# Second attention of a two-layer kernel: the incoming rows are added by GpSimd, not by TensorE

## The chip, the cores and the metric

One core of one Trainium2 chip runs the whole program. The metric is the device time of one execution in microseconds (us), lower is better.

## What is computed

Two layers over 8 x 512 tokens of width 256. Each is an attention and a feed-forward part, both read the same normalised rows, and both are added to the incoming rows. The second layer's attention is a gated linear recurrence over time, run over 4 batches of 1,024 tokens, 8 heads of 32:

```
xn = _layernorm(x, axis=-1)
x = x + _L1_attn_ref(xn, ...) + _L1_ffn_ref(xn, ...)

# in _L1_attn_ref
h = x * rsqrt(mean(x * x) + 1e-06) * norm_w
q, k, v = (heads(Wq), heads(Wk), heads(Wv))        # rope on q and k
beta, ig, og = sigmoid gates per token and head
def step(M, inp):
    M = M * f_t + g_t * scale * (k_t outer v_t)
    y_t = (q_t @ M) * o_t
return einsum('bld,ed->ble', y, Wout) + bout
```

The feed-forward part of the second layer is a mixture of 8 experts of width 1,024 with the two best chosen for each token.

## The kernel before, in words

The engines' queues are written out by hand. A list of steps (`plan2`, built by `shared_order` and `second_order`) is walked by each engine, which takes the steps that are its own. Order between engines is by semaphores, each counted up by its producer.

The second attention runs in chunks of 128 tokens, 32 of them, in the order `ORDER1`: the first chunk of each batch of 512, then the second of each, and so on. One pass over the tuple `TURN` is one turn, and the number behind a kind says which chunk it treats relative to the turn's own. In a turn, TensorE makes the value product (`project_val`, L1823, bank 3), the q/k product of the next chunk (`project_qk`, L1811), turns q and k (`turn`, L1839, and L1847 for the second gated q), makes the state products of the chunk before (`keys`, L1881 and L1887), its causal part (`update`, L1897), the scores (`affinity`, L1865, banks 2 to 5), and last the output projection of the chunk before (`project_out`, L1906 to L1910, bank 1). VectorE makes the rope (L2406, L2417, L2418), scans the decays of a chunk (`decay`, L2426, both inputs in SBUF), weighs the scores with them (`weigh`, L2433, PSUM and one SBUF input) and renews the state (L2445, 16 chunks). ScalarE copies and scales: values (L1369), turned q and k (L1376, L1381), the update's sum (L1387), keys (L1405), and the output sums (`out_copy`, L1410).

The rows `ACC` hold the sums of the first layer, 256 values a token. `project_out` starts its bank with the product identity x `ACC` row (L1906), adds the products with `WOUT` (L1909, after the semaphore `yt_put`, which ScalarE's L1387 gives) and the bias (L1910); ScalarE then writes the bank back into `ACC` and gives `oe_put`. The sync engine stores finished quarters of `ACC` (`store_sums`, L859). After the loop, TensorE's experts wait for all `oe_put`.

GpSimd multiplies the rotated q by the gates (`open`, L1082, and from the ninth chunk on L1088). From the routing on it also scatters the routing table of the experts into DRAM, 64 indirect DMAs (`scatter`, L978), three in a turn from the ninth turn on, put into the step `route`, ahead of `open` in the turn. After the last turn it gathers rows for the experts (`first_rows`, L1005), where `rows` stands in the list ahead of the last `out_copy`. TensorE turns the gathered rows (L1685).

Of the kernel before, what the change touches and what calls it, by code (L numbers as in the profile page):

```python
# [309 lines left out]
def build(nc, t, out):  # L310
    ctx = ExitStack()
    with ctx:
# [144 lines left out]
        WT = view(carve(1024), 1024).rearrange("p (g n) -> p g n", g=2)  # L457
        YT = view(carve(256), 256)
        top[0] = max(top[0], hs_at + 2048)
        FV = view(carve(256), 256)  # L460
# [133 lines left out]
        zero0, zero1 = sem("zero_xs0"), sem("zero_rest")  # L594
        b_in, b_cut, b_rows = sem("b_in"), sem("b_cut"), sem("b_rows")
        b1_turned, b1_put = sem("b1_turned"), sem("b1_put")
# [38 lines left out]
        kd_put, y_made, yt_put, dm_made, m_put = (sem(n) for n in ("kd_put", "y_made", "yt_put", "dm_made", "m_put"))  # L635
        out_made, oe_put, sums_out = (sem(n) for n in ("out_made", "oe_put", "sums_out"))

        xt_ready = {b: [(banks0[f"xt{c}", b][0], banks0[f"xt{c}", b][1] + 1) for c in range(2)] for b in range(NB)}
# [41 lines left out]
        def sync(sp):  # L680
# [113 lines left out]
            for k in range(3):  # L794
                sp.dma_start(B2S[8 * k:8 * k + 8, :], b3[0:8, k, :]).then_inc(b_rows, 16)
            attention_over(sp)
            sp.wait_ge(b_rows, 48)
            sp.wait_ge(b1_turned, 1)
# [58 lines left out]
            def store_sums(c):  # L857
                sp.wait_ge(oe_put, 8 * c + 8)
                sp.dma_start(ov[c], ACC.rearrange("p (b i) d -> p i b d", b=NB)[:, c]).then_inc(sums_out, 16)  # L859
# [55 lines left out]
        def second_over(eng):  # L915
            eng.wait_ge(out_made, NT)
            eng.wait_ge(oe_put, NT)
            eng.wait_ge(m_put, NST)
            eng.wait_ge(w_put, NT)
            eng.wait_ge(slot_turned, 2)  # L920


        def gpsimd(pool):
# [151 lines left out]
            def open_gates(n):  # L1075
# [9 lines left out]
                if n >= NB:  # L1085
                    if n >= NB + 2:
                        pool.wait_ge(e_turned, n - NB - 1)
                    pool.tensor_tensor(h8(QE2[par]), QK2[par][:, 0:8, :], hb(EF[:, i, :]), ALU.mult).then_inc(qe_put)  # L1088

            def bias_split():  # L1090

# [18 lines left out]
            for kind, *a in plan2:  # L1110
                if kind == "sums":
                    sums(*a)
                elif kind == "weights":
                    weights()
                elif kind == "combine" and on_pool(a[0]):
                    combine(*a)
                elif kind == "const1":
                    const1()
                    bias_split()
                elif kind == "gates" and a[1] == 4:  # L1120
                    gates(a[0])
                elif kind == "open":
                    open_gates(*a)
                elif kind == "scatter":
                    scatter(1, *a)
                elif kind == "rows":
                    first_rows(1)
# [6 lines left out]
        def scalar(act):  # L1134
# [273 lines left out]
            def project_out(n):  # L1408
                act.wait_ge(out_made, n + 1)
                act.activation(ACC[:, ORDER1[n], :], ps(1, 256, 512), ACT.Copy).then_inc(oe_put)  # L1410

# [40 lines left out]
        def tensor(pe):  # L1452
# [251 lines left out]
            def expert_down(layer, i):  # L1704
# [5 lines left out]
                if i == 0:  # L1710
                    pe.wait_ge(b_rows, 48)
                    pe.wait_ge(wd_in, 64 + 128 * layer)
# [187 lines left out]
            def project_out(n):  # L1900
# [3 lines left out]
                else:  # L1904
                    pe.wait_ge(const1_set, 12)
                pe.matmul(ps(1, 256, 512), ident, ACC[:, ORDER1[n], :], start=True, stop=False)  # L1906
                pe.wait_ge(yt_put, n + 1)
                for g in range(2):
                    pe.matmul(ps(1, 256, 512), YT[:, 128 * g:128 * g + 128], WOUT[:, g, :], start=False, stop=False)  # L1909
                pe.matmul(ps(1, 256, 512), ones3[0:96, :], BO3[0:96, :], start=False, stop=True).then_inc(out_made)  # L1910
# [653 lines left out]
```

## Time and profile before

| | |
|---|---|
| time, median of 3 runs | 1592.35 us (1588.64 to 1593.25) |
| profiled execution | 1598.56 us |
| span of its trace | 1596.8 us |
| TensorE busy | 1514.8 us (95%) |
| VectorE busy | 847.8 us (53%) |
| ScalarE busy | 746.2 us (47%) |
| GpSimd busy | 706.3 us (44%) |

The span is that of the trace; the profiled execution's own time lies a little above it. In the profile PE is TensorE's matmul, PEld its weight load, DVE VectorE, ACT ScalarE, POOL GpSimd and SPq the queue of the sync engine. L12 is line 12 of the kernel. A matmul in f32 shows as two records, one for each pass. Busy shares are means over stages with different limits, so that a wait is read in its stage. The second attention's turns run from about 860 to 1074 us of the span.

### The profile page before, as it was taken

Reading aid. Unit: us, or ns where it says so; the run is one execution under the profiler, and the core shown is the slowest. Engines: PE = TensorE matmul, PEld = TensorE weight load, DVE = VectorE, ACT = ScalarE, POOL = GpSimd, SP = SyncE. Lnnn points to the kernel's source line nnn. Section 1 sums busy time; section 2 is a strip of 40 time slices with the busy share of each in tenths; the row PEclk is TensorE's granted clock in tenths of the full one; section 3 lists DMA queues with packets and bytes.
Section 4 is the critical chain, followed back from the end, with each engine's and each line's share of the span. In section 5 each row is a group of like instructions: output and inputs, shape, how many; then the busy total and the mean of one; then the engine's idle time right before and its main releaser. Section 6 shows DMA issues by size and latency. Waiting matters only on the chain.

```text
span 1596.8 us, 32512 instructions
## 1 busy us (share of the span) xinstructions
PE 1514.8 (95%) x10874; PEld 1168.8 (73%) x10874; DVE 847.8 (53%) x2400; ACT 746.2 (47%) x1953; POOL 706.3 (44%) x815
## 2 busy tenths in 40 slices
PE   5988989999999999999987899999999999999997
PEld 3455545555548999997664577769999999999996
DVE  4777898888713444442577988874232222223230
ACT  4665655555641323323566676545333343343432
POOL 3232326667623555553710388852333433333331
PEclk9999999999999999999998999999999999999999
DMA  8534344555215444435621489647333333333331
GB/s 266 142 114 118 98 98 83 110 111 86 68 70 201 110 114 116 111 112 147 187 94 56 123 190 177 123 79 267 56 55 54 48 59 54 57 57 54 60 54 21
DMA packets 155835, 167.60 MB, mean 105 GB/s; under 512 B 84992, under 2 KB 132988, under 8 KB 153628
## 3 DMA queue, kind: packets, MB, share of 16 engines
q1 hardware_dynamic: 131132, 128.15, 32.8%
q0 software_dynamic: 24544, 37.38, 11.0%
q8 instruction: 94, 1.54, 0.4%
q14 instruction: 65, 0.53, 0.2%
HBM read 104.10 MB, written 44.45 MB: 93 GB/s over the span
## 4 chain that ended last, share of the span: by engine, by line
PE 81%; DVE 8%; ACT 3%; issue 3%; DMA 3%; SPq 1%; POOL 0%; DVEq 0%; another core or an unknown queue 0%; ACTq 0%; POOLq 0%
PE PS L1700 23%; PE PS L1718 23%; PE PS L1557 4%; PE PS L1521 3%; PE PS L1542 3%; PE PS L1811 3%; PE PS L1493 3%; PE PS L1674 2%; DVE PS L2023 2%; PE PS L1628 2%; PE PS L1823 2%; PE PS L1583 2%; PE PS L1909 1%; PE PS L1503 1%; ACT arena L1216 1%
## 5 line engine op out<-in xcount | busy, mean ns | idle before, releaser
L1700 PEld LDWEIGHTS PS<-arena 128*128 128x128 f32 x3408 | 396.6, 192 | 11.4
L1700 PE MATMUL PS<-arena 128*128 128x128 f32 x3408 | 403.1, 275 | 0.0
L1718 PE MATMUL PS<-arena 128*128 x1704 | 392.4, 379 | 0.8 <-ACT arena L1294 0.8
L1718 PEld LDWEIGHTS PS<-arena 128*128 128x128 f32 x1704 | 311.9, 190 | 41.1 <-issue 1.2
L2023 DVE CUSTOM_DVE_ANT_0 PS<-PS,arena 128x512 f32<-128x512 f32 (+3 forms) x512 | 235.5, 523 | 48.1 <-PE PS L1521 45.1
L1019 POOL DMA_INDIRECT out<-arena x71 | 111.6, 1571 | 299.4 <-ACT arena L1312 277.6
L1302 ACT ACTIVATE arena<-PS,arena 128x128 f32<-128x128 f32 x568 | 162.3, 369 | 134.6 <-PE PS L1700 132.9
L2276 DVE COPY arena<-arena 128x8 f32 x71 | 12.4, 174 | 353.3 <-ACT arena L1302 334.7
L1312 ACT ACTIVATE arena<-PS,arena 128x256 f32<-128x256 f32 x142 | 67.4, 475 | 256.8 <-PE PS L1720 177.6
L1005 POOL DMA_INDIRECT arena<-XN,arena x142 | 144.0, 1014 | 91.9 <-issue 38.4
L1216 ACT ACTIVATE arena<-PS 128x512 f32<-128x512 f32 (+1 forms) x256 | 166.0, 704 | 32.6 <-PE PS L1542 29.2
L952 POOL TENSOR_SCALAR_AFFINE_SELECT arena<-arena 128x256 f32<-128x256 f32 x256 | 98.4, 409 | 183.2 <-ACT arena L1216 182.0
L2277 DVE COPY arena<-arena 128x1024 f32 (+1 forms) x142 | 136.4, 961 | 73.0 <-ACT arena L1294 57.5
L978 POOL DMA_INDIRECT SLOT<-arena x128 | 156.6, 1223 | 28.5 <-issue 28.2
L1012 POOL DMA_INDIRECT SUM<-arena x71 | 70.6, 994 | 96.4 <-ACT arena L1312 96.4
L1521 PE MATMUL PS<-arena 96*128 96x512 bf16 (+3 forms) x512 | 100.8, 306 | 8.8 <-DVE arena L2023 6.8
L1542 PE MATMUL PS<-arena 99*128 99x512 bf16 (+3 forms) x512 | 96.4, 302 | 7.1 <-ACT arena L1216 5.9
L1294 ACT ACTIVATE arena<-PS 128x512 f32<-128x512 f32 x71 | 42.4, 598 | 113.6 <-issue 73.9
L1542 PEld LDWEIGHTS PS<-arena 99*128 99x128 bf16 x512 | 44.4, 98 | 57.7 <-issue 17.2
L1521 PEld LDWEIGHTS PS<-arena 96*128 96x128 bf16 x512 | 48.4, 98 | 51.5 <-DVE arena L2023 16.9
L2265 DVE COPY arena<-arena 128x512 uint16<-128x512 uint16 x126 | 53.9, 428 | 60.0 <-DMA arena<-XN,arena 57.9
L1557 PE MATMUL PS<-arena 128*32 128x512 f32 (+3 forms) x1024 | 75.7, 435 | 0.5 <-issue 0.4
(248 smaller groups left out, 1993.9 us busy)
## 6 DMA issues: line engine op xcount, KB each, us to landing
arena<-FD SPq DMA_DIRECT2D x32, 512.0 KB
SPL<-arena SPq DMA_DIRECT2D x32, 384.0 KB, 3.4
arena<-SPL SPq DMA_DIRECT2D x64, 192.0 KB
XN<-arena SPq DMA_DIRECT2D x16, 512.0 KB, 3.2
arena<-SPL SPq DMA_DIRECT2D x64, 128.0 KB
arena<-SUM SPq DMA_DIRECT2D x16, 512.0 KB, 6.4
arena<-in_w SPq DMA_DIRECT2D x16, 512.0 KB
arena<-in_w SPq DMA_DIRECT2D x8, 1024.0 KB
```

Of the source, the lines that this page charges most:

```text
L978: pool.indirect_dma_start(SLOT[layer], bass.IndirectOffsetOnAxis(ap=POS[:, n, i:i + 1], axis=0), META[:, i, n, :], None).then_inc(row_out[ ...
L1005: pool.indirect_dma_start(MOE[layer].xr[i % 4][:, :], None, XN, row).then_inc(tile_in[i % 4], 16)
L1019: pool.indirect_dma_start(out, row, m.y[i % 3][:, :], None, compute_op=ALU.add).then_inc(y_out[i % 3], 16)
L1216: act.activation(PB[h % NPB][:, lo:hi], ps(3, lo, hi), ACT.Exp, scale=0.25).then_inc(p_made)
L1302: ins = act.activation(m.hT[i % len(m.hT)][:, 128 * f:128 * f + 128], ps(m.UPB[i % 2], 128 * f, 128 * f + 128), ACT.Gelu, bias=m.bias[i % ...
L1521: ins = pe.matmul(ps(0, o, o + w), q[0:96, j, 128 * i:128 * i + 128], k[0:96, j, 0:w], start=True, stop=True)
L1542: ins = pe.matmul(ps(3, o, o + w), k[0:99, j, 128 * kb:128 * kb + 128], q[0:99, j, 128 * kb:512], start=True, stop=True)
L1557: ins = pe.matmul(PS[32 * j:32 * j + 32, 6, 128 * kb:512], vb[:, kb, 8 * half + jj, :], PB[(8 * n + jj) % NPB][:, OFFT[kb]:OFFT[kb] + w], ...
L1700: ins = pe.matmul(o, m.now[i % 2][:, c * F + 128 * f:c * F + 128 * f + 128], m.xt[i % 2][:, 128 * c:128 * c + 128], start=(c == 0), stop=( ...
L1718: ins = pe.matmul(to, m.hT[i % len(m.hT)][:, 128 * c:128 * c + 128], m.WD[:, bass.ds(e * (nf * 256) + c * 256, 256)], start=(c == 0), stop ...
L2023: dve.tensor_tensor_reduce(sc, sc, MASK[:, 384 - 128 * r:512], -1.0, -NEG, ALU.add, ALU.min, NM[n % 2][:, r, j:j + 1]).then_inc(s_max)
L2277: dve.tensor_copy(m.now[i % 2][:, :], m.WU[:, bass.ds(e * m.wrow, m.wrow)]).then_inc(w_staged)
```

## The change

The identity product is gone: the first product with `WOUT` opens the bank. ScalarE copies the bank into a new buffer `OB` of 256 values instead of into `ACC`, and GpSimd adds `OB` to the row of `ACC` (`add_out`, at the place of `out_copy` in its queue) and gives the new semaphore `row_added`. ScalarE's next copy waits for the addition before it, and the stores of the sums and the end of the stage wait for `row_added` in place of `oe_put`. The semaphore `b_rows` is merged into `b_in`. The whole diff:

```
--- before.py
+++ after.py
@@ -456,6 +456,7 @@
         QKT = view(carve(512), 512).rearrange("p (g k n) -> p g k n", g=2, k=2)
         WT = view(carve(1024), 1024).rearrange("p (g n) -> p g n", g=2)
         YT = view(carve(256), 256)
+        OB = view(carve(256), 256)
         top[0] = max(top[0], hs_at + 2048)
         FV = view(carve(256), 256)
         FT = view(carve(256), 256).rearrange("p (k n) -> p k n", k=2)
@@ -592,7 +593,7 @@
         st_made, p_made, o_made = sem("st_made"), sem("p_made"), sem("o_made")
         o_turned, o_recip, o_back, proj_made = sem("o_turned"), sem("o_recip"), sem("o_back"), sem("proj_made")
         zero0, zero1 = sem("zero_xs0"), sem("zero_rest")
-        b_in, b_cut, b_rows = sem("b_in"), sem("b_cut"), sem("b_rows")
+        b_in, b_cut = sem("b_in"), sem("b_cut")
         b1_turned, b1_put = sem("b1_turned"), sem("b1_put")
 
         r_step = sem("r_step")
@@ -634,6 +635,7 @@
         q_turned, e_turned, qk_put, qet_put, aff_made, w_put = (sem(n) for n in ("q_turned", "e_turned", "qk_put", "qet_put", "aff_made", "w_put"))
         kd_put, y_made, yt_put, dm_made, m_put = (sem(n) for n in ("kd_put", "y_made", "yt_put", "dm_made", "m_put"))
         out_made, oe_put, sums_out = (sem(n) for n in ("out_made", "oe_put", "sums_out"))
+        row_added = sem("row_added")
 
         xt_ready = {b: [(banks0[f"xt{c}", b][0], banks0[f"xt{c}", b][1] + 1) for c in range(2)] for b in range(NB)}
         wo_in_bank = banks0["output", NB - 1, 1]
@@ -792,9 +794,9 @@
 
             sp.wait_ge(b_cut, 6)
             for k in range(3):
-                sp.dma_start(B2S[8 * k:8 * k + 8, :], b3[0:8, k, :]).then_inc(b_rows, 16)
+                sp.dma_start(B2S[8 * k:8 * k + 8, :], b3[0:8, k, :]).then_inc(b_in, 16)
             attention_over(sp)
-            sp.wait_ge(b_rows, 48)
+            sp.wait_ge(b_in, 80)
             sp.wait_ge(b1_turned, 1)
             for q in range(4):
                 sp.dma_start(WU0[:, 2048 * q:2048 * q + 2048], t["Wu"][:, 2048 * q:2048 * q + 2048]).then_inc(wu_in, 16)
@@ -855,7 +857,7 @@
             ov = out[0:T, :].rearrange("(b i p) d -> i p b d", b=NB, p=128)
 
             def store_sums(c):
-                sp.wait_ge(oe_put, 8 * c + 8)
+                sp.wait_ge(row_added, 8 * c + 8)
                 sp.dma_start(ov[c], ACC.rearrange("p (b i) d -> p i b d", b=NB)[:, c]).then_inc(sums_out, 16)
 
             for kind, *a in plan2:
@@ -914,7 +916,7 @@
 
         def second_over(eng):
             eng.wait_ge(out_made, NT)
-            eng.wait_ge(oe_put, NT)
+            eng.wait_ge(row_added, NT)
             eng.wait_ge(m_put, NST)
             eng.wait_ge(w_put, NT)
             eng.wait_ge(slot_turned, 2)
@@ -1086,6 +1088,11 @@
                     if n >= NB + 2:
                         pool.wait_ge(e_turned, n - NB - 1)
                     pool.tensor_tensor(h8(QE2[par]), QK2[par][:, 0:8, :], hb(EF[:, i, :]), ALU.mult).then_inc(qe_put)
+
+            def add_out(n):
+                row = ACC[:, ORDER1[n], :]
+                pool.wait_ge(oe_put, n + 1)
+                pool.tensor_tensor(row, OB, row, ALU.add).then_inc(row_added)
 
             def bias_split():
 
@@ -1123,6 +1130,8 @@
                     open_gates(*a)
                 elif kind == "scatter":
                     scatter(1, *a)
+                elif kind == "out_copy":
+                    add_out(*a)
                 elif kind == "rows":
                     first_rows(1)
 
@@ -1407,7 +1416,9 @@
 
             def project_out(n):
                 act.wait_ge(out_made, n + 1)
-                act.activation(ACC[:, ORDER1[n], :], ps(1, 256, 512), ACT.Copy).then_inc(oe_put)
+                if n:
+                    act.wait_ge(row_added, n)
+                act.activation(OB, ps(1, 256, 512), ACT.Copy).then_inc(oe_put)
 
             for kind, *a in plan2:
                 if kind == "shared_up":
@@ -1708,7 +1719,7 @@
                 if i >= 2:
                     pe.wait_ge(y_put, NTILE * layer + i - 1)
                 if i == 0:
-                    pe.wait_ge(b_rows, 48)
+                    pe.wait_ge(b_in, 80)
                     pe.wait_ge(wd_in, 64 + 128 * layer)
                     if layer:
                         pe.wait_ge(l1_in, 176)
@@ -1903,10 +1914,9 @@
                     pe.wait_ge(oe_put, n)
                 else:
                     pe.wait_ge(const1_set, 12)
-                pe.matmul(ps(1, 256, 512), ident, ACC[:, ORDER1[n], :], start=True, stop=False)
                 pe.wait_ge(yt_put, n + 1)
                 for g in range(2):
-                    pe.matmul(ps(1, 256, 512), YT[:, 128 * g:128 * g + 128], WOUT[:, g, :], start=False, stop=False)
+                    pe.matmul(ps(1, 256, 512), YT[:, 128 * g:128 * g + 128], WOUT[:, g, :], start=(g == 0), stop=False)
                 pe.matmul(ps(1, 256, 512), ones3[0:96, :], BO3[0:96, :], start=False, stop=True).then_inc(out_made)
 
             for kind, *a in plan2:
```

## Rows read from the trace of the kernel before

**Rows 1.** The page: chain of work that ended last, by engine.
```profile
PE 81%; DVE 8%; ACT 3%; issue 3%; DMA 3%; SPq 1%; POOL 0%; DVEq 0%; another core or an unknown queue 0%; ACTq 0%; POOLq 0%
```
**Rows 2.** Groups, 850 to 1078 us: line, count, busy us, mean ns, idle before.
```profile
L1906 PE MATMUL PS<-arena 128*128 128x256 f32 x64 | 22.3, 429 | 0.0
...
L2445 DVE SCALAR_TENSOR_TENSOR arena<-arena,PS 128x128 f32<-128x128 f32 x32 | 9.6, 341 | 0.0
```
**Rows 3.** The chain in order of time: start us, us, what.
```profile
995.03 0.63 PE PS L1906 x2
```
**Rows 4.** One turn in order of time: start us, us, what, idle before.
```profile
1001.91 1.23 DVE L2433 TENSOR_TENSOR arena<-PS,arena 128x1024 f32<-128x1024 f32 x1 [0.43 <-PE PS L1865]
...
1002.91 1.01 POOL L978 DMA_INDIRECT SLOT<-arena  x1 [0.16 <-issue]
...
1003.32 1.07 PE L1823 MATMUL PS<-arena 128*128 128x256 f32 x4
1003.55 0.36 ACT L1410 ACTIVATE arena<-PS 128x256 f32<-128x256 f32 x1
1003.57 2.28 DVE L2426 TENSOR_TENSOR_SCAN arena<-arena 128x1024 f32<-128x1024 f32 x1
...
1004.22 2.40 POOL L978 DMA_INDIRECT SLOT<-arena  x1 [0.30 <-issue]
...
1005.94 0.60 PE L1839 MATMUL PS<-arena 128*128 128x128 f32 x4
...
1006.38 0.38 PE L1847 MATMUL PS<-arena 128*128 128x128 f32 x2
...
1006.93 0.96 POOL L978 DMA_INDIRECT SLOT<-arena  x1 [0.31 <-issue]
...
1007.28 0.62 PE L1897 MATMUL PS<-arena 128*32 128x128 f32 x16
...
1008.41 0.38 ACT L1387 ACTIVATE arena<-PS 128x256 f32<-128x256 f32 x1 [0.96 <-PE PS L1897]
1008.42 0.61 POOL L1082 TENSOR_TENSOR arena<-arena 128x256 f32<-128x256 f32 x1 [0.52 <-DVE arena L2418]
...
1008.74 1.23 DVE L2433 TENSOR_TENSOR arena<-PS,arena 128x1024 f32<-128x1024 f32 x1 [0.41 <-PE PS L1865]
...
1008.99 0.61 POOL L1088 TENSOR_TENSOR arena<-arena 128x256 f32<-128x256 f32 x1
...
1010.08 0.73 PEld L1823 LDWEIGHTS PS<-arena 128*128 128x128 f32 x4 [0.17 <-issue]
```
**Rows 5.** Order of time, 820 to 832 us, GpSimd and VectorE.
```profile
820.72 0.19 DVE L2331 TENSOR_TENSOR arena<-arena 128x32 f32<-128x32 f32 x1
...
826.57 2.23 DVE L2426 TENSOR_TENSOR_SCAN arena<-arena 128x1024 f32<-128x1024 f32 x1
...
828.36 2.60 POOL L1053 TENSOR_TENSOR arena<-arena 128x1024 f32<-128x1024 f32 x1 [25.68 <-DMA arena<-SUM]
...
829.61 1.40 DVE L2331 TENSOR_TENSOR arena<-arena 128x32 f32<-128x32 f32 x1
```
**Rows 6.** Order of time, end of the second attention.
```profile
1069.57 1.00 POOL L1005 DMA_INDIRECT arena<-XN,arena  x1 [4.76 <-DVE arena L2201]
...
1071.03 0.38 ACT L1410 ACTIVATE arena<-PS 128x256 f32<-128x256 f32 x1 [2.24 <-PE PS L1910]
...
1075.30 0.41 PE L1685 MATMUL PS<-arena 128*128 128x128 f32 x2 [0.61 <-DVE arena L2251]
```
**Rows 7.** Order of time, a turn at 909 to 914 us.
```profile
910.14 0.96 POOL L978 DMA_INDIRECT SLOT<-arena  x1 [0.30 <-PE PS L1839]
...
910.39 0.62 PE L1897 MATMUL PS<-arena 128*32 128x128 f32 x16
...
911.41 0.97 POOL L978 DMA_INDIRECT SLOT<-arena  x1 [0.30 <-issue]
...
913.02 0.38 ACT L1387 ACTIVATE arena<-PS 128x256 f32<-128x256 f32 x1 [2.02 <-remote]
```

More of the change, by code:

```diff
@@ L458, in build @@
         YT = view(carve(256), 256)
+        OB = view(carve(256), 256)
         top[0] = max(top[0], hs_at + 2048)
@@ L594, in build @@
         zero0, zero1 = sem("zero_xs0"), sem("zero_rest")
-        b_in, b_cut, b_rows = sem("b_in"), sem("b_cut"), sem("b_rows")
+        b_in, b_cut = sem("b_in"), sem("b_cut")
         b1_turned, b1_put = sem("b1_turned"), sem("b1_put")
@@ L636, in build @@
         out_made, oe_put, sums_out = (sem(n) for n in ("out_made", "oe_put", "sums_out"))
+        row_added = sem("row_added")
         xt_ready = {b: [(banks0[f"xt{c}", b][0], banks0[f"xt{c}", b][1] + 1) for c in range(2)] for b in range(NB)}
@@ L794, in sync @@
             for k in range(3):
-                sp.dma_start(B2S[8 * k:8 * k + 8, :], b3[0:8, k, :]).then_inc(b_rows, 16)
+                sp.dma_start(B2S[8 * k:8 * k + 8, :], b3[0:8, k, :]).then_inc(b_in, 16)
             attention_over(sp)
-            sp.wait_ge(b_rows, 48)
+            sp.wait_ge(b_in, 80)
             sp.wait_ge(b1_turned, 1)
@@ L857, in store_sums @@
             def store_sums(c):
-                sp.wait_ge(oe_put, 8 * c + 8)
+                sp.wait_ge(row_added, 8 * c + 8)
                 sp.dma_start(ov[c], ACC.rearrange("p (b i) d -> p i b d", b=NB)[:, c]).then_inc(sums_out, 16)
@@ L916, in second_over @@
             eng.wait_ge(out_made, NT)
-            eng.wait_ge(oe_put, NT)
+            eng.wait_ge(row_added, NT)
             eng.wait_ge(m_put, NST)
@@ L1088, in open_gates, with add_out @@
                     pool.tensor_tensor(h8(QE2[par]), QK2[par][:, 0:8, :], hb(EF[:, i, :]), ALU.mult).then_inc(qe_put)
+            def add_out(n):
+                row = ACC[:, ORDER1[n], :]
+                pool.wait_ge(oe_put, n + 1)
+                pool.tensor_tensor(row, OB, row, ALU.add).then_inc(row_added)
             def bias_split():
@@ L1125, in gpsimd @@
                     scatter(1, *a)
+                elif kind == "out_copy":
+                    add_out(*a)
                 elif kind == "rows":
@@ L1409, in project_out @@
                 act.wait_ge(out_made, n + 1)
-                act.activation(ACC[:, ORDER1[n], :], ps(1, 256, 512), ACT.Copy).then_inc(oe_put)
+                if n:
+                    act.wait_ge(row_added, n)
+                act.activation(OB, ps(1, 256, 512), ACT.Copy).then_inc(oe_put)
             for kind, *a in plan2:
@@ L1710, in expert_down @@
                 if i == 0:
-                    pe.wait_ge(b_rows, 48)
+                    pe.wait_ge(b_in, 80)
                     pe.wait_ge(wd_in, 64 + 128 * layer)
@@ L1905, in project_out @@
                     pe.wait_ge(const1_set, 12)
-                pe.matmul(ps(1, 256, 512), ident, ACC[:, ORDER1[n], :], start=True, stop=False)
                 pe.wait_ge(yt_put, n + 1)
                 for g in range(2):
-                    pe.matmul(ps(1, 256, 512), YT[:, 128 * g:128 * g + 128], WOUT[:, g, :], start=False, stop=False)
+                    pe.matmul(ps(1, 256, 512), YT[:, 128 * g:128 * g + 128], WOUT[:, g, :], start=(g == 0), stop=False)
                 pe.matmul(ps(1, 256, 512), ones3[0:96, :], BO3[0:96, :], start=False, stop=True).then_inc(out_made)
```

## Prediction

> **What bounds the kernel now.** I read the page first. TensorE makes up 81% of the chain of work that ended last [rows 1], so taking products off TensorE looks like a pure gain. The second attention decides, and there I went to its groups, its chain, and then one turn in order of time. The groups give the prize: the identity product is 64 records (two passes for each of 32 products), 22.3 us busy [rows 2]. The chain shows that its two passes take 0.63 us of each turn (995.03 to 995.66), right ahead of the output product [rows 3]. A program that only shortened TensorE's queue would gain 32 x 0.63 = 20 us.
>
> The turn in order of time says otherwise. I count from the end of VectorE's weighing (L2433), which is 1001.91 + 1.23 = 1003.14; the next ends at 1008.74 + 1.23 = 1009.97, so a turn is 6.83 us. TensorE's load for the value product (L1823) starts at 1010.08, 0.11 after that end, and its product 0.18 after one, 1003.32 against 1003.14 [rows 4]. The load follows the weighing's end, not TensorE's own queue: what comes 0.11 after an end is what was released by it. The value product waits for the weighing, because both use the score banks. So the ring weighing, value product, q/k product, turns, state products, scores, weighing is the bound. The output projection lies outside the ring, beside the weighing, which takes 1.23 us anyway. Between the load's start and the product's lie 0.07 us in which the array may still be full. What lies under the weighing is worth at most these 0.07 us a turn, not 0.63.
>
> GpSimd's turn is the other thing to see. It holds three scatters of slots (L978) and two gate products (L1082, L1088), 0.61 each, and waits only 0.52 for VectorE's rope (L2418) [rows 4]. Two of the scatters take 1.01 and 0.96; the middle one takes 2.40 [rows 4].
>
> **Why it takes that long** decides the cost. The scan (L2426) runs 1003.57 to 1005.85. The scatter that starts inside it ends at 6.62, 0.77 after it. It is a 0.96 us scatter of which 0.19 had passed when it was stopped. A plain sum does the same: L1053 starts at 828.36 inside a scan that ends at 828.80 and itself ends at 830.96. In turn VectorE's L2331 (two inputs in SBUF, 0.19 at 820.72) takes 1.40 when it starts at 829.61 inside that L1053, and ends 0.05 after it [rows 5]. So a GpSimd sum and a VectorE instruction with two SBUF inputs exclude each other, and whoever comes second waits.
>
> The Trainium skill has this exclusion (SBUF — State Buffer, section Who interferes with whom: a VectorE instruction with two SBUF inputs contends with a GpSimd instruction that reads SBUF, and the later one blocks fully), and the rows agree. Its section A bandwidth-pool intuition that's wrong has what is blocked end about 115 ns after VectorE. The trace has 0.77 us for a scatter. By 0.115 instead of the 0.42 used below a locked turn would cost 0.3 us less, and the sum would be 4 us less.
>
> **The change, part by part.** Times are from the end of the weighing.
>
> *Removed:* 64 passes, 0.63 us a turn, of which at most 0.07 is on the ring, and nothing of it where GpSimd sets the pace. The output product would then wait for the copy of the update (L1387), which is nearly ready.
>
> *OB, the waits and the merged semaphore:* ScalarE's copy keeps its shape (L1410, 0.36 [rows 4]). Its new wait is for the addition a whole turn before, done some 5 us earlier, so it costs nothing until GpSimd is a turn late. b_in for b_rows waits for the same loads: nothing.
>
> *Added:* 32 additions of 128x256, each 0.61 like L1082 and 0.57 behind one another, the step from L1082 to L1088 [rows 4]. The place is what costs. The addition stands in GpSimd's queue behind the gate products of the next turn and ahead of the three scatters of the next. The gate products end at -0.37 (9.60 against 9.97). The copy ends at 1003.55 + 0.36 = 0.77. The scan starts at 0.43 and ends at 2.71. So the addition waits for the copy, runs into the scan and ends at 2.71 + 0.42 = 3.13 (0.42 is 0.61 less the 0.19 already passed). Behind it the scatters, unstretched now, take 0.16 + 3 x 0.96 + 2 x 0.30 = 3.64, to 6.77. The gate products could start at 5.28; they start at 6.80, 1.5 late.
>
> *Does the slack hold it?* TensorE needs q for its turn (L1839) at 2.80 and the second product for L1847 at 3.24, one turn after GpSimd makes them. Less 0.18, as between the weighing and its product: 2.62 and 3.06. Today they are ready at -0.94 and -0.37, a slack of some 3.5 us. The second late turn: first product 6.80 - 6.83 = -0.03 to 0.58, second stopped by the scan, which itself slips to about 2.8, ready 3.2: 0.15 late. Then addition to 3.8, scatters to 7.4, which is 0.5 in the next turn, past the scan's start at 0.43. From there it is locked: both products behind the scan, 3.13 and 3.70. The second is 0.64 late, the turn is 7.47, the addition ends 4.27, the scatters 7.91, or 0.44 of the next turn. The product that follows at 0.47 would be stopped 0.19 later, when the scan (0.43) has long begun. GpSimd's slack of 3.5 us is used up not by its own length but by the scan, once a turn.
>
> *Sum.* The state's update (L2445), which puts the scan at 0.43, is in 32/2 = 16 turns [rows 2]. The first costs nothing, the second 0.15, 14 cost 0.64: 9.1 us. The scatters go on for some four turns without that update. There the scan starts half a us earlier, so the second product is ready at 3.2 against 3.06: 0.5 us together. The first eight turns have no scatters, but VectorE sets their pace there and an addition can hold it up to 0.6: between 0 and 5 us, I take 1, since most of them fall beside the weighing, which reads PSUM and one SBUF input. At the end the addition of the last row but one stands ahead of the gathers of the experts' first rows. They start at 1069.57 today; the copy at 1071.03 + 0.38 [rows 6], 0.6 less for the removed product, plus 0.61 gives 1071.5. TensorE turns the second tile at 1075.30 and waits for such a gather up to then, so 1 to 1.9 us, I take 1.5. The store of the last sums goes out 3.5 us later than today; the experts' first two tiles need neither it nor the weights behind it, and cover it. If they did not, it would cost those 3.5. Removed: -0.3, for the turns that are not locked. Sum 9.1 + 0.5 + 1 + 1.5 - 0.3 = +11.8 us. The profiled execution (1598.56, span 1596.8) is 6 us above the median; the difference is put on the median: 1592.35 + 11.8 = 1604.
>
> **Rivals.**
>
> *Late reports.* In some turns the copy of the update (L1387) starts long after its products. In the usual turn it starts 1.13 after the first of them (1007.28, 1008.41) [rows 4]. In the turn at 910.39, with scatters begun 0.25 before and 1.02 after that, it starts 2.63 after, at 913.02 [rows 7]. I can't say why, but it goes with scatters that fall upon these products, and the weighing follows. In the locked turn these products start at 4.14 + 0.64 = 4.78 and scatters at 4.43 and 5.69, 0.35 before and 0.91 after: like 910.39. The copy would be at 4.78 + 2.63 = 7.41, 1.50 behind the 5.91 of a usual turn so shifted. If the weighing is as late, it adds 1.5 a turn, for 14 turns 21 us: 1625. With half of that, 1614. Against it: such turns are few in the trace, and the scores, which the weighing also needs, come later than the copy, so that a part is hidden. Chance 0.25, most of it between 1608 and 1628.
>
> *Absorbed.* The lock needs the next product to reach the point at which it can be stopped after 0.43; it does by 0.23. If GpSimd is 0.25 us quicker, or the addition slips in ahead of the scan, the products stay within the 3.5 us of slack, and only ends are left: +1 to +3, 1594 to 1596. Chance 0.14.
>
> *Faster.* The chain puts all of the 0.63 on the path. It would come if the weighing did not release the value product. What decides is how long after the weighing TensorE would be free without the removed passes: the output products would have to end later than the weighing by themselves for the 0.63 to count. At most it is 20 us, 1572. The rows speak against it. Chance 0.04.
>
> **Numbers.** Forecast as worked out (1597 to 1609) 0.57, late reports 0.25, absorbed 0.14, faster 0.04. A measurement of this kernel tells 0.3%, 4.8 us, from no change: slower means above 1597.1. The late reports and nearly all of the forecast lie there: 0.81. Same: absorbed, and the forecast's low edge, 0.15. Faster 0.04. The range takes in the absorbed case and the late reports: 1594 to 1628.
>
> **What the profile would show.** Additions of 2 to 2.6 us that end 0.42 after the scan, scatters of 0.96 each, gate products stopped by the scan too, TensorE's idle time ahead of L1847 put down to L1088, turns of 7.3 to 7.5 with scatters, and VectorE's wait for scores longer. L1823's load still 0.11 behind the weighing. I am wrong if the gate products end before -0.3 in most turns (absorbed), if L1823 starts well before 0.1 after a weighing's end, or if turns reach 8 us (late reports).

## The result, and the profile after

The changed kernel takes 1612.24 us (1608.69 to 1613.11) against 1592.8: ratio 1.0114, 95% interval 1.0096 to 1.0132. That is slower by 1.1%, 19.4 us between the medians. It lies inside the stated range of 1594 to 1628, but above the 1597 to 1609 in which the forecast as worked out was to fall. The profiled executions lie closer, 1613.11 and 1598.56 (+14.6; spans 1611.4 and 1596.8); where the other 4.8 us are is part of what follows.

The groups of the trace after, 850 to 1100 us (line, count, busy us, mean ns, idle before):

```profile
L2436 DVE TENSOR_TENSOR_SCAN arena<-arena 128x1024 f32<-128x1024 f32 x30 | 71.8, 2392 | 0.0
L980 POOL DMA_INDIRECT SLOT<-arena x64 | 63.2, 988 | 16.4 <-issue 16.4
L1084 POOL TENSOR_TENSOR arena<-arena 128x256 f32<-128x256 f32 x30 | 55.6, 1854 | 52.1 <-DVE arena L2428 51.7
...
L1834 PE MATMUL PS<-arena 128*128 128x256 f32 x120 | 34.7, 414 | 13.0 <-DVE arena L2443 13.0
L1095 POOL TENSOR_TENSOR arena<-arena 128x256 f32<-128x256 f32 x32 | 30.2, 945 | 8.8 <-ACT arena L1421 8.8
```

The additions (L1095) themselves are not what grew most: their mean is 945 ns. The first gate product (L1084) takes 1854 ns in the mean, against 610 where nobody stops it [rows 4], and the scatters (L980) are now all of about 0.96 us: the middle one took 2.40 before [rows 4]. What the scan stops is now another instruction, the gate product. One turn in order of time (start us, us, what, idle before) shows it:

```profile
935.28 1.23 DVE L2443 TENSOR_TENSOR arena<-PS,arena 128x1024 f32<-128x1024 f32 x1 [1.11 <-PE PS L1876]
...
936.93 2.47 DVE L2436 TENSOR_TENSOR_SCAN arena<-arena 128x1024 f32<-128x1024 f32 x1
937.27 2.54 POOL L1084 TENSOR_TENSOR arena<-arena 128x256 f32<-128x256 f32 x1
...
939.77 0.61 POOL L1090 TENSOR_TENSOR arena<-arena 128x256 f32<-128x256 f32 x1
...
939.91 0.63 PE L1850 MATMUL PS<-arena 128*128 128x128 f32 x4 [0.44 <-issue]
940.35 0.72 POOL L1095 TENSOR_TENSOR arena<-arena 128x256 f32<-128x256 f32 x1
...
941.23 1.01 POOL L980 DMA_INDIRECT SLOT<-arena  x1 [0.16 <-issue]
...
941.41 0.62 PE L1908 MATMUL PS<-arena 128*32 128x128 f32 x16
942.10 0.38 ACT L1396 ACTIVATE arena<-PS 128x256 f32<-128x256 f32 x1 [0.66 <-PE PS L1908]
942.54 0.96 POOL L980 DMA_INDIRECT SLOT<-arena  x1 [0.30 <-issue]
942.76 1.22 DVE L2443 TENSOR_TENSOR arena<-PS,arena 128x1024 f32<-128x1024 f32 x1 [1.07 <-PE PS L1876]
```

The weighing ends at 936.51 and again at 943.98: 7.47. (A figure with a plus, here and below, is a time in us from the end of a weighing.) The gate product starts in the scan and ends at 939.81, 0.41 after the scan's 939.40. TensorE's turn of q (L1850) starts 0.10 after that, at +3.40 from the weighing where it was +2.80. Then GpSimd runs without a pause till the next scan: its own queue now takes longer for a turn than TensorE and VectorE would, and sets the pace. Such turns are called locked below. The 16 turns from 921.46 to 1042.17 take 7.54 each, against 6.82 before (921.12 to 1030.21).

Cut at the ends of weighings, the two traces differ by -2.5 us up to the first weighing, +3.9 from the first weighing to the eighth (57.8 to 61.7; all figures for the first turns below are this distance), +8.9 over the next 16, +0.4 to the last weighing and +3.9 behind it (526.1 to 530.0): +14.6.

### The profile page after: what moved, and what is told of

Read it like the earlier page. It is cut to its first block, busy times and chain, and to the rows that moved or that the text cites. A ratio compares the mean times of both kernels' runs of the same rounds, so it can differ in the third digit from the quotient of the medians.

```text
span 1611.4 us, 32479 instructions
## 1 busy us (share of the span) xinstructions
PE 1513.7 (94%) x10810; PEld 1155.0 (72%) x10810; DVE 854.7 (53%) x2400; ACT 746.5 (46%) x1953; POOL 741.0 (46%) x847
## 4 chain that ended last, share of the span: by engine, by line
PE 79%; DVE 9%; issue 4%; DMA 3%; ACT 2%; SPq 2%; POOL 1%; DVEq 0%; ACTq 0%; POOLq 0%
PE PS L1711 23%; PE PS L1729 23%; PE PS L1568 3%; PE PS L1532 3%; PE PS L1553 3%; PE PS L1822 3%; PE PS L1504 3%; DVE arena L2443 2%; PE PS L1639 2%; PE PS L1685 2%; PE PS L1834 2%; DVE PS L2033 2%; SPq L731 2%; PE PS L1594 2%; PE PS L1514 1%
## 5 line engine op out<-in xcount | busy, mean ns | idle before, releaser
L980 POOL DMA_INDIRECT SLOT<-arena x128 | 126.0, 984 | 28.6 <-issue 28.6
L1084 POOL TENSOR_TENSOR arena<-arena 128x256 f32<-128x256 f32 x32 | 56.9, 1777 | 67.2 <-DVE arena L2428 66.8
L2275 DVE COPY arena<-arena 128x512 uint16<-128x512 uint16 x126 | 54.3, 431 | 62.8 <-DMA arena<-XN,arena 62.7
```

Of the source, the lines that this page charges most:

```text
L980: pool.indirect_dma_start(SLOT[layer], bass.IndirectOffsetOnAxis(ap=POS[:, n, i:i + 1], axis=0), META[:, i, n, :], None).then_inc(row_out[ ...
```

## Experiments

Three sets of four kernels ran on three chips, each set beside the kernel before on the same chip, whose medians were 1599.07, 1593.27 and 1600.01. Each kernel was traced once. Ratios are against the kernel before of the same set. The code shows the lines that matter; ` ...` stands for the rest of an edit.

**Set 1. The identity product alone is taken out.** One line less; the incoming rows are left out.

```
-  pe.matmul(ps(1, 256, 512), ident, ACC[:, ORDER1[n], :], start=True, stop=False)
 ...
   for g in range(2):
-      pe.matmul(..., start=False, stop=False)
+      pe.matmul(..., start=(g == 0), stop=False)
```

> The kernel before with the identity product taken out and nothing put in its place (this leaves out the addition of the incoming rows). My theory: the product lies under the weighing, so its removal gives at most 0.07 us in each of some 20 full turns, and turns of 6.8 us stay; with TensorE idle longer in the first eight turns its granted clock can fall to half for a turn, as it did in the changed kernel, which costs about 1 us each time. Expected 1590 to 1595 us, the same as before within 0.3%. The rival, that the chain's 0.63 us a turn is on the path, expects 1572 to 1578. A second question is the late report of the update's sum: if it comes from scatters alone, the copy of the update still starts 1.1 us after the first product in full turns and over 2 in the turns with a scatter right behind it; if it needs the identity product, it starts 0.7 us after in all.

1600.7 us, ratio 1.0001 (0.9987 to 1.0015). The removal is worth nothing: the 16 turns take 6.81. The late reports are there without the product too. One thing came with it that the sum had at nothing: the sixth turn takes 8.02 us for 6.77, at a granted clock of 0.64, and the first turns 59.4 in place of 57.8.

**The addition alone is put in**, 32 sums of GpSimd's that nobody reads, the identity product kept.

```
-  pool.tensor_tensor(row, OB, row, ALU.add).then_inc(row_added)
+  pool.tensor_tensor(OB, row, row, ALU.add).then_inc(row_added)
 ...                                       # copy and identity product as before
```

> The kernel before, identity product and copy kept, with 32 additions of 128x256 on GpSimd at the place where the change has them and with the same waits; their result is not used. My theory: the cost of the change is GpSimd's alone, by the scan that stops the addition and then, one turn later, the gate products. Expected the changed kernel's turns of 7.4 to 7.7 us and 1609 to 1615 us, with gate products of about 2.5 us. The rival, that the wait of ScalarE's copy for the addition or the single buffer OB costs the time, expects 1592 to 1597, since that wait is not here. If late reports come from scatters with an identity product, turns are longer than in the changed kernel, up to 8.8, and the time up to 1630.

1642.48 us, ratio 1.027 (1.0253 to 1.0287), far above what I expected and above the change itself. The turns take 9.05, yet no gate product is stopped: ScalarE's copy of the update starts 1.9 to 3.5 us behind the update's first product where 0.69 would do. It is the late report of the rivals, larger than there.

**The addition is put behind the scatters**, right ahead of the gate products; the gathers of the experts' first rows then stand ahead of the last two additions.

```
   elif kind == "open":
+      if late: add_out(late.pop())
       open_gates(*a)
   elif kind == "out_copy":
-      add_out(*a)
 ...
+      late.append(a[0])
```

> The changed kernel with one edit: the addition stands behind the scatters of the next turn, right ahead of the gate products, and the gathers of the experts' first rows go ahead of the last two additions. The same 32 additions, not one instruction less. My theory: a scatter is now what is stopped by the scan, as before the change, the addition runs at 4.8 to 5.4 us after the weighing with no scan near it, and the gate products start 0.1 late, with 3.5 us of slack. Expected turns of 6.8 us, additions of 0.6 to 0.7 us, and 1590 to 1598 us (first eight turns still 1 to 3 us longer than before, by additions that stop VectorE and a lower clock). The rival, that GpSimd is simply too long with 0.61 us more in a turn in which it waits 0.52, expects 6.9 to 7.1 us a turn and 1596 to 1600.

1613.02 us, ratio 1.0084 (1.0064 to 1.0104); 7.15 a turn, not 6.8. A turn of it in order of time:

```profile
978.09 0.96 POOL L980 DMA_INDIRECT SLOT<-arena  x1 [0.30 <-issue]
...
978.72 0.73 DVE L2433 TENSOR_TENSOR arena<-arena 128x256 f32<-128x256 f32 x1
979.08 0.95 POOL L1095 TENSOR_TENSOR arena<-arena 128x256 f32<-128x256 f32 x1
979.37 0.94 DVE L2434 TENSOR_TENSOR arena<-arena 128x256 f32<-128x256 f32 x1
980.24 1.21 DVE L2449 TENSOR_TENSOR arena<-PS,arena 128x1024 f32<-128x1024 f32 x1
```

Now the addition meets the two rope sums, which take 0.73 and 0.94 in place of 0.43 and 0.42. VectorE pays, the weighing comes later, and the gate products wait 0.36 for the rope. The exclusion holds in both directions; moving the addition chose who waits. It did not lock here: no gate product was stopped, and GpSimd's turn less its wait is 7.15 - 0.36 = 6.79.

**VectorE adds the rows**, straight from the bank, behind the weighing; no copy, no GpSimd.

```
+  dve.wait_ge(out_made, n + 1)
+  dve.tensor_tensor(row, ps(1, 256, 512), row, ALU.add).then_inc(oe_put)
 ...                                       # identity product and ScalarE's copy go
```

> The kernel before without the identity product and without ScalarE's copy: VectorE adds the bank to the row of the sums, one instruction behind the weighing, PSUM and one SBUF input, so that it neither stops GpSimd nor is stopped. VectorE's turn has 0.36 us of idle time ahead of the rope and 0.4 ahead of the weighing; the addition takes about 0.42 and pushes the scan. My theory (the ring is bound by weighing, products and scores): turns of 6.8 to 6.95 us, 1589 to 1598 us, no gain to speak of. If TensorE's length were the bound: 1573 to 1578.

1604.2 us, ratio 1.0031 (1.0022 to 1.0041): the best of those that compute the whole without the product, and still not better than with it. Its turns take 6.91, its first turns 62.8.

**Set 2. The addition between the second and third scatter.**

```
   elif kind == "scatter":
       scatter(1, *a)
+      late[0][1] += 1                     # late is filled at out_copy
+      if late[0][1] == 2: add_out(late.pop()[0])
```

> The changed kernel, its additions only moved in GpSimd's queue: behind the turn's second scatter and ahead of its third, all else as in the change. Lock theory (a GpSimd sum of two tiles of the on-chip memory and a VectorE instruction with two such operands exclude each other, and 9 to 12 us of the change's cost is one addition held by the scan, with the gate products and scatters pushed behind it): in the steady turns the second scatter still ends 0.6 us behind the scan, at about +3.5 us from the weighing's end; the addition starts there, beside the rope product that reads one operand from TensorE's banks, and takes 0.61 to 0.75 us; the third scatter is at about +4.4, the gate products at +5.3 to +5.5, VectorE's own instructions keep their lengths, and the turns are 6.8 to 6.9 us, in place of 7.5 behind the change and 7.15 with the addition behind all three scatters. With the first eight turns and the tail as in the change (+4 and +4 us): about 1.003 to 1.005 of the time before. Rival (what costs is any work of GpSimd's between the output copy and the gate products, wherever it stands): turns of 7.15 or more, ratio 1.008 or more. The extra question is the late report: if it takes two scatters right behind each other, TensorE's report behind the update is on time (ScalarE's copy 0.7 us behind the update's first product, not 1.1).

1612.71 us, ratio 1.0111 (1.0089 to 1.0133). My expectation fell. The turns lock all the same at 7.44, with additions at +6.3 and the first gate product stopped at +0.75 for 2.50. Moving it by two scatters does not help, because GpSimd's turn is nearly full, as the next run shows.

**Fills in place of the addition**, same wait and report; the incoming rows are left out.

```
-  pool.tensor_tensor(row, OB, row, ALU.add).then_inc(row_added)
+  pool.memset(OB, 0.0)
+  pool.memset(row, 0.0).then_inc(row_added)
```

> The changed kernel with the addition replaced by two fills of 256 columns at the same place, with the same wait and the same report (it leaves out the incoming rows, so its output is the fill). They read nothing. Theory (the lock is over reading two operands): the fills are not held by the scan; they run from about +0.1 to +0.4 us behind the weighing and take 0.2 to 0.4 us each, the gate products follow right behind them only if their input is ready (it is, as before: then +5.3), the scatters stand where they did before, and the steady turns are 6.8 to 6.9 us; ratio 1.000 to 1.003. Rival 1 (any GpSimd access to the memory beside a two-operand VectorE instruction excludes it): the second fill or both end some 0.3 us behind the scan, turns 7.3 or more, ratio 1.007 or more. Rival 2 (the wait for the output copy, not the addition, is what costs): turns as in the change, 7.5.

1598.89 us, ratio 1.0039 (1.0024 to 1.0054). A turn in order of time:

```profile
972.35 2.37 DVE L2437 TENSOR_TENSOR_SCAN arena<-arena 128x1024 f32<-128x1024 f32 x1
972.49 0.32 POOL L1095 MEMSET arena<- 128x256 f32 x1
972.75 0.31 POOL L1096 MEMSET arena<- 128x256 f32 x1
973.23 2.31 POOL L980 DMA_INDIRECT SLOT<-arena  x1 [0.17 <-issue]
...
976.06 0.62 PE L1909 MATMUL PS<-arena 128*32 128x128 f32 x16
976.75 0.38 ACT L1397 ACTIVATE arena<-PS 128x256 f32<-128x256 f32 x1 [0.52 <-PE PS L1909]
```

Both fills run inside the scan at their own length: this scan doesn't stop what reads nothing. (VectorE's copies of 128x2048 do: beside two of them, at the end of the stage, the first of a pair of fills took 1.09 and 1.31.) The turns are 6.71 or 6.72, but for one of 8.21 and the last few: shorter than the 6.83 of before, and the copy of the update is on time. But GpSimd's turn is now 6.73, and from 945 us on its gate products slip by some 0.02 a turn, until after twelve turns one of them reaches the scan and is stopped (2.62 us, next turn 7.01). The two fills cost GpSimd 0.6 a turn and fill it to the brim. An addition costs 0.72, so in either of the two places in which it was tried beside reports on time it spills over. What the fills do cost lies at the ends: the first turns take 59.4 and the tail, from the last weighing to the end, 529.3, where the gathers wait for the fills.

**The gathers ahead of the last two additions.**

```
   elif kind == "out_copy":
-      add_out(*a)
+      if a[0] < NT - 2: add_out(*a)
 ...
+  add_out(NT - 2); add_out(NT - 1)      # behind first_rows(1)
```

> The changed kernel, with only the last two additions moved behind the eight gathers of the expert layer's first rows in GpSimd's queue. Theory (the tail's +3.9 us comes of the gathers held by the last additions, about 1.5 us directly, and of TensorE's clock falling while it waits for the gathered rows): gathers begin within 0.3 us of the slots being written, as before; the first product of the experts is at about +4.6 us from the last weighing in place of +6, the granted clock there is as before, and the end is 3 to 4 us earlier than in the change: ratio 1.009. Rival (the tail's loss lies elsewhere, in the store of the sums or in the layer's weights, which wait for the last additions): the tail stays 530 us and the ratio 1.011.

1614.53 us, ratio 1.0134 (1.0115 to 1.0154); the tail stays at 529.7. The end of it in order of time:

```profile
1080.75 1.00 POOL L1007 DMA_INDIRECT arena<-XN,arena  x1 [1.91 <-DVE arena L2214]
...
1086.40 0.73 POOL L1095 TENSOR_TENSOR arena<-arena 128x256 f32<-128x256 f32 x1
...
1087.22 0.38 ACT L1424 ACTIVATE arena<-PS 128x256 f32<-128x256 f32 x1 [4.01 <-POOL arena L1095]
...
1087.71 0.41 PE L1699 MATMUL PS<-arena 128*128 128x128 f32 x2 [3.14 <-issue]
```

The gathers start on time, but with one buffer the last copy waits 4.01 us for the addition before it, and TensorE's experts wait for that copy. The wait only moved.

**The identity product kept, into an unused half bank.**

```
+  pe.matmul(ps(1, 0, 256), ident, ACC[:, ORDER1[n], :], start=True, stop=True)
```

> The changed kernel with the identity product still done by TensorE, into an idle half of the bank, where nobody reads it. It tells what the removal alone gives when the addition is there. By the forecast the removal is worth 0.07 us a turn at most, and nothing in the turns that the addition's lock sets, since TensorE waits there for the gate products: ratio 1.011 to 1.013. Sub-question, the clock: in the turn in which TensorE waits 2.3 us for the weighing and its granted clock then falls (one turn of 7.92 us for 6.8), the product stands in front of that wait and not in it, so the clock falls all the same. Rival (the removed 0.3 us of work per turn is what lets the clock fall): that turn is back at 6.8 to 7.2 us and the ratio 1.010 or less.

1614.99 us, ratio 1.0122 (1.01 to 1.0145); 7.52 a turn. The product costs nothing here either, and the turn with the fallen clock, described further down, is there with it (8.02 us).

**Set 3. The change for rows 8 to 29 only.**

```
+  def on_pe(n): return n < 8 or n >= NT - 2     # the identity product as before
 ...
```

> The change for rows 8 to 29 alone; rows 0 to 7 and the last two are added by TensorE's identity product as before. Theory (the cost is a sum of three parts that don't depend on each other: the locked turns, the first eight turns, and the tail): the first eight turns are back at 57.8 to 59.4 us in place of 61.7, the tail at about 526.1 in place of 530.0, the steady turns stay at 7.4 to 7.6 us, and the cost is what the trace of the change has between the eighth and the last weighing, +9.3 us: ratio 1.006 (1.004 to 1.008). Rival (the lock needs the late start that the first turns give it): steady turns of 6.8 and a ratio of 1.002 or less.

1639.32 us, ratio 1.0239 (1.0208 to 1.027). The ends are back: 57.7 and 526.15 us. The middle is not the locked turn but one of 9.19:

```profile
957.29 2.28 DVE L2452 TENSOR_TENSOR_SCAN arena<-arena 128x1024 f32<-128x1024 f32 x1
957.71 2.38 POOL L1106 TENSOR_TENSOR arena<-arena 128x256 f32<-128x256 f32 x1 [2.08 <-ACT arena L1435]
960.25 1.00 POOL L989 DMA_INDIRECT SLOT<-arena  x1 [0.16 <-issue]
...
961.01 0.62 PE L1922 MATMUL PS<-arena 128*32 128x128 f32 x16
...
962.86 0.96 POOL L989 DMA_INDIRECT SLOT<-arena  x1 [0.30 <-issue]
...
964.50 0.38 ACT L1407 ACTIVATE arena<-PS 128x256 f32<-128x256 f32 x1 [3.33 <-remote]
```

The update's products run at 961.01, and ScalarE hears of them at 964.50, 0.68 after the third scatter has ended.

**The counterpart, rows 0 to 7 and the last two.**

```
+  def on_pe(n): return 8 <= n < NT - 2
 ...
```

> The counterpart: rows 0 to 7 and the last two are added by GpSimd, rows 8 to 29 by TensorE's identity product. Theory of the three parts: first eight turns 61 to 62 us, the 16 steady turns 6.8 us with the late reports of before, tail 529 to 530 us: +7.8 us, ratio 1.005 (1.003 to 1.007); its excess and that of the run with the middle alone add up to the change's 1.011. Rival (the additions at the ends lie beside other waits): ratio within 0.002 of 1.

1609.41 us, ratio 1.0059 (1.0039 to 1.0079); first turns 60.4, tail 528.8. In the very turn where the addition first meets scatters, it gives the pair that tells most. Here it is in this kernel:

```profile
909.97 2.71 POOL L1106 TENSOR_TENSOR arena<-arena 128x256 f32<-128x256 f32 x1
912.84 1.05 POOL L989 DMA_INDIRECT SLOT<-arena  x1 [0.16 <-issue]
...
913.57 0.62 PE L1922 MATMUL PS<-arena 128*32 128x128 f32 x16
914.20 0.96 POOL L989 DMA_INDIRECT SLOT<-arena  x1 [0.30 <-issue]
915.46 0.96 POOL L989 DMA_INDIRECT SLOT<-arena  x1 [0.30 <-issue]
...
915.62 0.26 PE L1890 MATMUL PS<-arena 32*128 32x128 f32 x1 [0.24 <-issue]
...
917.19 0.38 ACT L1407 ACTIVATE arena<-PS 128x256 f32<-128x256 f32 x1 [3.00 <-remote]
...
917.35 1.23 DVE L2459 TENSOR_TENSOR arena<-PS,arena 128x1024 f32<-128x1024 f32 x1 [2.28 <-PE PS L1890]
```

and here in the changed kernel, whose weighing ends 1.80 earlier:

```profile
908.17 2.71 POOL L1095 TENSOR_TENSOR arena<-arena 128x256 f32<-128x256 f32 x1
911.04 1.05 POOL L980 DMA_INDIRECT SLOT<-arena  x1 [0.16 <-issue]
...
911.77 0.62 PE L1908 MATMUL PS<-arena 128*32 128x128 f32 x16
912.40 0.96 POOL L980 DMA_INDIRECT SLOT<-arena  x1 [0.30 <-issue]
912.46 0.38 ACT L1396 ACTIVATE arena<-PS 128x256 f32<-128x256 f32 x1
```

Up to the second scatter every start is the same to 0.01, 1.80 apart, and the copy is 3.62 behind the products in one and 0.69 in the other. So neither the order nor the timing of what ran before makes a report late. Nor is it ScalarE that is slow to hear: VectorE's weighing, which waits for TensorE too, starts 1.47 behind the end of the last score product (915.88), against 0.06 in the changed kernel. TensorE's work is held up as well: the score products take 1.55 from first to last in one and 0.73 in the other.

**The gathers first, and a buffer of its own for the last row.**

```
-  act.activation(OB, ps(1, 256, 512), ACT.Copy)
+  act.activation(OBL if n == NT - 1 else OB, ps(1, 256, 512), ACT.Copy)
 ...
```

> The additions of the last two rows behind the eight gathers once more, now with a buffer of its own for the last row's sums, so that ScalarE's last copy, for which TensorE's first product of the experts waits, doesn't wait for the addition before it. In the run without that buffer the copy waited 4.0 us and the tail stayed at 529.7. Theory: the first product over gathered rows is at +3.6 us from the last weighing, as before (it was +4.8 in the change and +5.9 in the run before), TensorE's idle time ahead of it is under 1.5 us and the tail 526 to 527 us; ratio 1.009 with the rest as in the change. Rival (the tail hangs on the store of the sums and on the 8 MB of weights behind it, which wait for the last addition at about +5 us in place of +3.6): tail 528 or more.

1646.57 us, ratio 1.0278 (1.0237 to 1.032). The first expert product comes at +3.29 from the last weighing, but both additions then hold the fifth gather, TensorE waits 1.82 for the third tile, and the tail is 528.2: half of the loss is gone, and neither theory holds whole. The middle is the same code as in the run of set 2 without this buffer, which took 7.53 a turn at 1.0134; here it takes 9.12.

**One fill in the kernel before.**

```
+  pool.wait_ge(oe_put, n + 1)
 ...
+  pool.memset(OB, 0.0).then_inc(row_added)      # OB is read by nobody, n < 30
```

> The kernel before, its identity product kept, with one fill of an unused 256-column tile on GpSimd at the place of the change's addition, behind the same wait (0.31 us each in the run with fills). It adds work and leaves nothing out. In three runs with an operation of GpSimd's right ahead of the turn's scatters TensorE's reports were on time, and in three runs with none there they came 0.4 to 2.1 us late. Theory (the place of the first scatter decides): the copy behind the update starts 0.7 us behind its first product in all turns, the turns are 6.70 to 6.75 us in place of 6.83, the three turns of 7.5 to 7.7 us are gone, and the time is 2 to 4 us under before: ratio 0.998. Rival (the on-time reports came of the removed identity product or of the copy into the buffer): reports late as before, ratio 1.000 to 1.002.

1620.47 us, ratio 1.0121 (1.0087 to 1.0154). The theory that the place of the first scatter decides is gone: the copy is 2.5 us behind in most turns, which take 8.04. So where reports come late, one fill of 0.31 us can cost 1.2 us a turn.

## Why the prediction was right, and where its sizes were off

*The removal.* "At most 0.07 us a turn": shown. Without the product 1.0001; with it, beside the addition, 7.52 against 7.54. The load stayed 0.11 to 0.12 behind the weighing in the full turns of ten of the fourteen kernels, before and after the change among them. In the other four, all with late reports, it came up to 0.99 behind it in some turns.

*The exclusion and the lock.* Shown. The locked turn was to be 7.47; it is 7.40 to 7.77, since the scan gets longer as well (2392 ns against 2.28 [rows 4]). A gate product that is stopped ends 0.41 behind the scan, where the sum had 0.42. 16 turns cost 11.6 us where I had 9.1. The fills show that the scan excludes what reads, the rope sums that VectorE pays as well. What I had not seen is how little room GpSimd's turn has, some 0.6 us: between the scatters the addition locks as ahead of them. From the eighth to the last weighing the traces differ by 9.3 us, just what the terms for this part come to (9.1 + 0.5 - 0.3), but that is luck: the 2.5 too little for the locked turns is made up by late reports in the trace of before, as told below.

*The first eight turns.* The term was +1 and is +3.9, the worst miss of the sum. In the two runs with the same additions whose clock did not fall in the sixth turn (the gathers first, with one buffer and with two) they take 59.5, +1.7: an addition beside VectorE's short sums costs 0.2 to 0.5 in five of seven turns. The rest goes with the clock, which the sum had at nothing. In the changed kernel TensorE waits 2.33 us for a weighing (1.50 before), and then

```profile
892.80 2.04 PE L1834 MATMUL PS<-arena 128*128 128x256 f32 x4 [2.33 <-DVE arena L2443]
```

takes 2.04 in place of 1.10, as at the lower of the clock's two levels, 1.2 for 2.4 GHz. The view by stretches (from and to, length, busy us and count of PE, PEld, DVE, ACT and POOL, then PEclk, DMA share, GB/s) has a granted clock of 0.64 there, against 1.00 in the same stretch before:

```profile
892.50:897.20 4.70, 4.40 (x10) 2.65 (x11) 3.90 (x5) 1.54 (x8) 0.40 (x1) 0.64 0.31 115
```

That turn is 7.92 where it was 6.77. The first turn is 9.35 for 8.42 in the run with the gathers first, at 0.72 for 0.80. The wait alone doesn't decide: in that same run TensorE waits 2.33 too, the clock stays at 1.00, and the turn takes 6.97. And the additions aren't needed: without product or addition it waits 1.93 and the clock is 0.64. Of the nine kernels without the product in the first eight turns, seven take 7.8 to 8.0 in the sixth turn and two 7.0; of the five with it, four take 6.8 to 6.9 and one 8.0. So the fall goes mostly with the removal, and what brings it on stays open.

*The tail.* +1.5 was predicted and +3.9 came. The place was right, the gathers behind the addition. The end of the changed kernel in order of time:

```profile
1081.76 1.40 POOL L1095 TENSOR_TENSOR arena<-arena 128x256 f32<-128x256 f32 x1 [3.41 <-ACT arena L1421]
1083.32 1.00 POOL L1007 DMA_INDIRECT arena<-XN,arena  x1 [0.16 <-issue]
...
1086.16 0.41 PE L1696 MATMUL PS<-arena 128*128 128x128 f32 x2 [2.06 <-DMA arena<-XN,arena]
...
1087.39 0.69 PE L1696 MATMUL PS<-arena 128*128 128x128 f32 x2 [0.82 <-DMA arena<-XN,arena]
...
1088.12 1.77 POOL L1095 TENSOR_TENSOR arena<-arena 128x256 f32<-128x256 f32 x1
```

The first sum already took 1.40, beside a copy of VectorE's, so the gathers began at 1083.32, +1.95 from the last weighing where they had begun at -1.11 [rows 6]. TensorE waited 2.06 and 0.82, its clock fell again (0.74 from 1088 to 1093 us), and the second addition held the fifth gather. With the last two rows back on TensorE the tail is 526.15: all of it comes with these two additions. Fills in the same place cost 3.1.

*Late reports*, the rival at 0.25, are real, and larger than I had made them, but they did not come in the changed kernel's trace: that its 1612 lies near the rival's "with half of that, 1614" is chance. In the turns from the eighth to the twenty-eighth, 21 in all, the copy started more than 0.75 us behind the update's first product in 12 to 21 of them in each of the eight kernels of sets 1 and 3, and in none in the four of set 2 and in the changed kernel's trace; in the trace of before it was 19 of 21. The state goes with the set and not with the code: the two runs with the gathers first have the same code in these turns and stand on opposite sides. A set is one chip at one time, so which of the two decides can't be told. That also orders the medians of the kernel before: 1599 and 1600 us in the sets with late reports, 1593 in the one without, and 1592.8 beside the changed kernel, while its profiled execution, with late reports, took 1598.56. I take it that this one execution was in the other state, which is argued and not shown: the kernel before was never traced with reports on time. The sum speaks for it: late reports cost it 0.11 in each of 16 turns (6.83 against 6.72) and 1.25, 0.91 and 0.86 in three others, 4.8 us; 14.6 + 4.8 = 19.4, the difference of the medians, though single executions of the kernel before lie 6 us apart there. So the forecast of 11.8 was short by 7.6: 4.8 of this, 2.9 in the first turns, 2.4 in the tail and 2.5 in the locked turns, less the 2.5 by which the stage happened to begin earlier and the 2.6 of late turns that the traces already count as a gain.

What the change costs where reports come late was not measured with the changed kernel itself. The two kernels nearest to it took 1.0239 and 1.0278 there. What makes a report late stays open.

## What to carry to other kernels

Before moving work to an idle-looking engine, add up that engine's turn, stops by the exclusion included, against the turn that sets the pace; if the rest is less than the work, its place in the queue only chooses who waits (7.5 us a turn ahead of the scatters, 7.15 behind them, in place of 6.8). Taking an instruction off the busiest engine gives nothing while what follows it is released by another engine: look how long after a release it starts. Compare only traces taken on the same chip at the same time, and look first whether they share such states: the pair here differed by late reports worth 5 us, a quarter of what was to be explained.

## What the runs showed of the hardware

- TensorE's reports came late in two sets and on time in another, in one pair with all starts before them equal. Where they were late, the copy that waits for them started 0.3 to 0.9 us after the end of one of GpSimd's scatters in 161 of 172 turns: scatters ending at +4.75, +6.07 and +6.96 gave the copy at +5.25, +6.65 and +7.6.
- A fill of GpSimd's (0.31 us) is not stopped by a two-operand scan, but beside VectorE's copy of 128x2048 it took 1.09 and 1.31. A scatter, a sum of two tiles and a gate product are stopped by the scan and end 0.4 to 0.8 us after it. The scan itself grew from 2.28 to as much as 2.60 in the changed kernel.
- After a wait of 2.33 us the granted clock was 0.64 of full over the next 4.7 us in the changed kernel, and 1.00 in the run with the gathers first; after 1.93 it was 0.64 without the identity product, after 1.50 it was 1.00 before. The turn took 7.9 to 8.0 us at 0.64 and 6.8 to 7.0 at 1.00.
